# Fetching the first items' rows into buffers and later rows on top of positions in x, with reordered first steps

## The chip, the cores and the metric

One core of a Trainium2 chip runs the whole program. The time is what the device takes for one execution, in microseconds (us); of the kernel before three executions were timed, 1590.24, 1590.33 and 1594.37 us, median 1590.33.

## What is computed

A small language-model tower over 32 sequences of 256 tokens with 192 features. The part that matters here is the first one: the embedding with positions and four layers of a selective-scan block.

```python
x = embedding[tokens] + pos_enc[:S][None]
for l in range(L):          # L = 4
    h = _layernorm(x, g, bt)
    uv = h @ Wi.T + bi                    # u, v
    uc = _dwconv_causal(u, cw, cb)        # 4 taps
    delta = softplus(uc @ wd.T + bd_)
    Bm, Cm = uc @ wB.T + bB_, uc @ wC.T + bC_
    y = _selective_scan(uc, delta, Bm, Cm)   # h = h * exp(-delta) + uc * Bm;  y = sum(h * Cm)
    x = x + ((y * sigmoid(v)) @ wo.T + bo)
```

An attention block with a partial rotary embedding and an int8 feed-forward layer follow; the change does not touch them.

## The kernel before

x stays on the chip for the whole program, 64 tiles of 128 tokens by 192 features. An **item** is four tiles, two sequences, in one layer; a layer has 16 items and the four layers 64, numbered through. Each engine runs its own program, and the programs are written as a software pipeline: step m works on several items at once, `at(lag)` being item m - lag. The helper `steps` writes the first six steps of a layer out, loops over pairs of steps, and writes the last ones out. The engines meet only at semaphores, and each engine takes its own instructions strictly in the order written.

What an item goes through, with its lag and its line: DVE measures mean and variance one step ahead (`statistics` L1424, `variance` L1439, lag -1); POOL computes the inverse deviation in seven small instructions (`inverse_deviation`, L479 to L491, lag -1); at lag 0 ACT rounds the scaled rows (`round_rows`, L1176), DVE makes what the rounding left (`rest_of_rows`, L1448) and POOL adds the output bias to the rows for later (`bias_rows`, L503). At lag 1 PE transposes them (L758) and ACT saves them (`save_turned`, L1166). At lag 2 PE makes u and v (`uv`, L697), ACT saves u and makes the convolution's first tap (L1116 to L1137), DVE adds the other three (`other_taps`, L1465), ACT rounds the result (`round_uc`, L1186 and L1189), DVE makes the rest (`rest_of_uc`, L1479 and L1474), and ACT makes the gates sigmoid(v) (`gates`, sv_l L1199 and sv_h L1202). PE's `uv` of the next item waits for those gates. At lag 3 come the decay on ACT (`decay`, L1147) and PE's products from uc (L706, L717); at lag 4 the recurrence on DVE (scans hs_h L1500 and hs_l L1509), the output product (L787) and the residual sum (L1537).

The rows of layer 0 come from DRAM. The table of token numbers is made by DVE and PE in the first 5 us. `index` (L414) copies four columns of it, `gather` (L419) issues four indirect transfers of 128 rows each from POOL's queue into a buffer `emb` (items 0 to 3 have buffers of their own, later ones take turns), and `place` adds the positions and writes x: on DVE (L1404) for items 0 to 3, on POOL (L437) for the others. POOL issues the gathers of the first four items one after the other, and only then computes item 0's inverse deviation. In its step it places item m + 2, copies the indices of m + 4 and gathers m + 3, ahead of `inverse_deviation` and `bias_rows`. Before the first step DVE scales and centres layer 0's weights (`centre_weights`, L1360), ACT rounds them (`round_weights`, L1103), and DVE makes their rests (L1380, L1383). SP's queue brings weights: w_o and the biases bo_row after the first two items' rows, other weights after six items, later layers' weights when their buffers are free.

```python
            for n in range(FIRST):
                wait(pool, s_idx4, n + 1)
                gather(n, n, n % 2)
...
            inverse_deviation(item(0))
```

## Time and profile before

| what | value |
|---|---|
| time, median of three | 1590.33 us |
| time of the profiled execution | 1598.23 us |
| its span | 1596.3 us |
| PE busy | 1506.3 us, 94% |
| DVE busy | 1349.4 us, 85% |
| ACT busy | 1241.8 us, 78% |
| POOL busy | 836.2 us, 52% |
| gathers, adding of positions on POOL | 64 transfers issued; 12 instructions |

Engines are PE (matmul), DVE (vector), ACT (scalar), POOL (GpSimd) and SP (the queue of plain transfers). Busy time is from start to end of the instructions of an engine, without the issuing of waits and registers. The profiled execution is one of its own; its time is 7.90 us above the median of the others, and its span leaves out 1.9 us of its time. In the 40 slices of the profile PE is busy over 90% of each from the third to the last but two, all but one of them, so an average over the span says little about the first 80 us, where PE stands in two slices at 20 and 60%. The rows below are therefore taken from short stretches.

### The profile page before, as it was taken

The page shows a single profiled execution, that of the slowest core. Times are in us where ns is not written, and L with a number is a line of the kernel's source. Part 1 is how long each engine was busy: PE and PEld are TensorE (multiplying, and loading weights), DVE is VectorE, ACT ScalarE, POOL GpSimd, SP SyncE. Part 2 cuts the span into 40 slices and gives each one's busy share as a digit, 9 for nine tenths or more (in the row PEclk, how much of TensorE's full clock was granted, in tenths as well). Part 3 has the DMA queues.
Part 4 walks back from the last instruction along what each step waited for, and adds up shares of the span by engine and source line. Part 5 has one row for each costly group of instructions (what it writes and reads, how often), then busy time and mean ns, then how long its engine had stood idle before and what let it go on. Part 6 is the DMA issues. An engine that isn't in the chain of part 4 may idle for free.

```text
span 1596.3 us, 36428 instructions
## 1 busy us (share of the span) xinstructions
PE 1506.3 (94%) x11313; PEld 1232.6 (77%) x11313; DVE 1349.4 (85%) x3201; ACT 1241.8 (78%) x2686; POOL 836.2 (52%) x1428
## 2 busy tenths in 40 slices
PE   2699999999999999999999998999999999999986
PEld 1588878888888888888888886677777777777763
DVE  4699999999999999999999886678888878888763
ACT  2688878888888888888888963777787877877762
POOL 7777755443334453333333236566666666666642
PEclk9799999999999999999999997999999999999996
DMA  5311100000000000000000000000000000000000
GB/s 111 80 29 30 30 23 34 1 34 0 0 1 1 1 1 0 0 1 1 1 1 0 1 1 1 2 8 12 12 10 15 11 11 10 10 10 15 11 12 25
DMA packets 16571, 22.41 MB, mean 14 GB/s; under 512 B 2912, under 2 KB 13792, under 8 KB 16480
## 3 DMA queue, kind: packets, MB, share of 16 engines
q1 hardware_dynamic: 13408, 14.98, 2.8%
q0 software_dynamic: 3072, 6.30, 2.6%
q8 instruction: 48, 0.79, 0.2%
q14 instruction: 43, 0.35, 0.1%
HBM read 14.58 MB, written 6.29 MB: 13 GB/s over the span
## 4 chain that ended last, share of the span: by engine, by line
PE 60%; DVE 18%; ACT 9%; issue 9%; POOL 2%; DMA 1%; DVEq 1%; ACTq 0%; POOLq 0%
PE banks L706 9%; PE banks L921 7%; PE banks L697 7%; PE banks L889 6%; PE banks L846 5%; PE banks L873 5%; PE banks L860 4%; DVE hs_h L1500 3%; DVE x L1537 3%; DVE xs L1448 2%; PE banks L787 2%; PE banks L717 2%; PE banks L832 2%; PE banks L945 2%; PE banks L835 2%
## 5 line engine op out<-in xcount | busy, mean ns | idle before, releaser
L1593 DVE TENSOR_REDUCE mx<-banks 128x4 f32<-128x1024 f32 x192 | 234.2, 1220 | 45.6 <-PE banks L860 45.1
L1224 ACT ACTIVATE probs<-banks 128x1024 f32<-128x1024 f32 x192 | 195.7, 1019 | 84.5 <-PE banks L873 81.1
L503 POOL TENSOR_TENSOR x<-x,bo_row 128x768 f32<-128x768 f32 (+1 forms) x64 | 118.3, 1848 | 159.0 <-DVE ucr_r L1474 159.0
L697 PE MATMUL banks<-ht,w_uv 128*128 128x512 f32 x576 | 166.3, 398 | 14.3 <-ACT sv_l L1199 12.5
L479 POOL TENSOR_TENSOR lnt<-mv,const 128x4 f32<-128x4 f32 x64 | 20.4, 319 | 269.1 <-DVE mv L1439 268.8
L1465 DVE SCALAR_TENSOR_TENSOR uc_h<-u_h,vec,uc_h 128x512 f32<-128x512 f32 x192 | 146.9, 765 | 0.9 <-ACT uc_h L1137 0.9
L697 PEld LDWEIGHTS banks<-ht,w_uv 128*128 128x128 f32 x576 | 108.4, 191 | 42.0 <-issue 18.1
L1448 DVE SCALAR_TENSOR_TENSOR xs<-x,rstd,xs 128x192 fp32r<-128x192 f32 x256 | 89.9, 413 | 46.5 <-ACT xs L1176 46.5
L697 PE MATMUL banks<-ht,w_uv_rest 128*128 128x512 f32 x384 | 120.0, 394 | 0.0
L1116 ACT ACTIVATE u_l<-banks,vec 64x256 f32<-64x256 f32 x128 | 60.0, 469 | 73.5 <-PE banks L697 72.7
L873 PE MATMUL banks<-q_t,k_t 64*128 64x256 f32 x768 | 108.8, 334 | 7.7 <-ACT probs L1224 6.3
L706 PE MATMUL banks<-ucr_h,w_z 128*128 128x512 f32 x256 | 107.6, 420 | 4.5 <-issue 2.8
L846 PE MATMUL banks<-identr,parts 128*128 128x128 f32 x768 | 105.0, 261 | 4.2 <-issue 3.3
L1465 DVE SCALAR_TENSOR_TENSOR uc_l<-u_l,vec,uc_l 128x256 f32<-128x256 f32 x192 | 95.2, 496 | 12.1 <-POOL rstd L491 3.9
L1166 ACT ACTIVATE ht<-banks 128x512 fp32r<-128x512 f32 x192 | 100.8, 598 | 5.0 <-PE banks L758 3.5
L889 PE MATMUL banks<-probs,v_aug 128*32 128x256 f32 x1536 | 104.5, 390 | 0.0
L1133 ACT ACTIVATE uc_l<-banks,vec 64x256 f32<-64x256 f32 x128 | 71.7, 560 | 42.1 <-DVE inp_l L1494 41.0
L758 PEld LDWEIGHTS banks<-identr,xs 128*128 128x128 f32 x768 | 74.5, 142 | 38.0 <-DVE xs L1448 19.1
L1176 ACT ACTIVATE xs<-x,rstd 128x192 fp32r<-128x192 f32 (+1 forms) x256 | 95.6, 445 | 9.9 <-POOL rstd L491 8.3
L758 PE MATMUL banks<-identr,xs 128*128 128x128 f32 x768 | 77.6, 247 | 27.2 <-DVE xs L1448 19.0
L860 PE MATMUL banks<-k_t,q_t 64*128 64x256 f32 x768 | 94.7, 303 | 6.6 <-DVE mx L1593 2.6
L706 PE MATMUL banks<-ucr_l,w_z 128*128 128x512 f32 x256 | 101.0, 394 | 0.0
(191 smaller groups left out, 4662.8 us busy)
## 6 DMA issues: line engine op xcount, KB each, us to landing
out_dram<-y_out SPq DMA_DIRECT2D x32, 192.0 KB, 2.0
raw_z<-w_z_dram SPq DMA_DIRECT2D x4, 704.0 KB, 5.3
raw_uv<-w_uv_dram SPq DMA_DIRECT2D x4, 576.0 KB, 3.9
emb<-embedding_dram,idx POOLq DMA_INDIRECT x64
q_t<-mx_t SPq DMA_DIRECT2D x64, 6.0 KB
emb<-w_qkv_dram SPq DMA_DIRECT2D x1, 864.0 KB
w_o<-w_o_dram SPq DMA_DIRECT2D x1, 768.0 KB
bo_row<-bout_dram SPq DMA_DIRECT2D x4, 96.0 KB
```

What stands on the lines that cost most here:

```text
L503: nc.gpsimd.tensor_tensor(rows, rows, bo_row[:, l, :][:, None, :].broadcast_to([P, CT, D]), ALU.add).then_inc(x_biased, 1)
L697: last = nc.tensor.matmul(out[:], w, r[:], start=(k == 0), stop=(k == len(passes) - 1))
L706: last = nc.tensor.matmul(out[:], w, r[:, b, :], start=(k == 0), stop=(k == len(passes) - 1))
L758: last = nc.tensor.transpose(B_T[g][:, k * P:(k + 1) * P].bitcast(F32R), xs[:, k, g * P:(g + 1) * P], identr[:])
L846: last = nc.tensor.transpose(B_HEADS[g][:, (2 * o + t) * P:(2 * o + t + 1) * P].bitcast(F32R), parts[:, s, t, o, 2 * g:2 * g + 2, :].rearr ...
L860: last = nc.tensor.matmul(B_S[j][:, t * S:(t + 1) * S], q_t[q, s, g, t * P:(t + 1) * P], k_t[q, s, g, :], start=True, stop=True)
L873: last = nc.tensor.matmul(B_ST[j][:, t * S:(t + 1) * S], k_t[q, s, g, t * P:(t + 1) * P], q_t[q, s, g, :], start=True, stop=True)
L889: last = nc.tensor.matmul(bank[32 * h:32 * h + 32, c:c + S], v_aug[:, s, t, 4 * p + h, :], probs[:, (s + p) % 2, h // 2, (2 * (h % 2) + t) ...
L1224: act.activation(probs[:, (s + g // 2) % 2, g % 2, :].rearrange("p (j k) -> p j k", j=2), B_SST, ACT.Exp, scale=float(DH) ** -0.5).then_in ...
L1448: last = nc.vector.scalar_tensor_tensor(out=xs[:, k, D:2 * D], in0=x[:, tile_of(c, k)], scalar=rstd[:, s, k:k + 1], in1=xs[:, k, 0:D].bitc ...
L1465: nc.vector.scalar_tensor_tensor(out=uc, in0=uk, scalar=v(l, part, V_W0 + k), in1=uc, op0=ALU.mult, op1=ALU.add).then_inc(taps, 1)
L1593: nc.vector.tensor_reduce(mx[:, s].rearrange("p t (j h) -> p j t h", j=2)[:, :, :, g], B_SS.rearrange("p j (t k) -> p j t k", t=2), AX, AL ...
```

## The change

Four things. **Rows:** the index copies go; each gather reads its indices from the table itself. Items 0 to 3 are gathered into buffers as before, and DVE adds their positions. For items 4 to 15 SP first writes the positions into x, a transfer within the chip's memory, and POOL's gather then adds the embedding rows to what stands there; `place` on POOL is gone. POOL's part of layer 0 is written out in full. **POOL's opening:** the inverse deviation of item 0 comes after two items' gathers, and the other fetches are spread over the steps. **First steps:** in steps 0 to 4 of layer 0 DVE has an order of its own, with the measuring of later items behind the taps, and in steps 0 to 3 ACT computes the gates before it rounds uc. ACT rounds item 0 before the first step, and the wait for the weights' rests is split in two. **Table and bias:** an activation of one column loads the sigmoid's table at the start; the bias for layer 0 is one transfer, those of the other layers are sent later, last before the later weights; in the first four items POOL's bias waits for one item of uc more.

```diff
+        def items_of(t, n):
+
+            return t[:, n * CT * D:(n + 1) * CT * D].rearrange("p (b d) -> p b d", b=2)
+
+        positions = pos[:].rearrange("p h d -> p (h d)")[:, None, :].broadcast_to([P, 2, 2 * D])
...
-        def steps(eng, step):
+        def steps(eng, step, fetches=False):
 
 
             LEAD = 6
             for l in range(L):
-                for k in range(LEAD):
+
+                for k in range(NCH if fetches and l == 0 else LEAD):
                     m = l * NCH + k
                     step(lambda lag, m=m: item(m - lag), l, k)
+                if fetches and l == 0:
+                    continue
...
-            for n in range(2):
-                sp.wait_ge(s_emb[n], 16 * CT)
+
+            def base(n):
+
+                s = n % 2
+                wait(sp, xs_ready, n - 5)
+                wait(sp, s_base[s], 8 * (n - s - FIRST))
+                sp.dma_start(items_of(x, n), positions).then_inc(s_base[s], 16)
+
+
+
+            sp.wait_ge(s_pos, 16)
+            base(FIRST)
+            sp.wait_ge(s_first[1], 16 * CT)
+            sp.dma_start(bo_row[:, 0, :], bout[0:1, :].broadcast_to([P, D])).then_inc(s_bo[0], 16)
+            base(FIRST + 1)
+            sp.wait_ge(s_first[3], 16 * CT)
             sp.dma_start(w_o[:], w_o_d).then_inc(s_wo, 16)
-            for i in range(L):
-                sp.dma_start(bo_row[:, i, :], bout[i:i + 1, :].broadcast_to([P, D])).then_inc(s_wo, 16)
-
-            sp.wait_ge(x_loaded, 6)
+            for n in range(FIRST + 2, 10):
+                base(n)
+            for i in range(1, L):
+                sp.dma_start(bo_row[:, i, :], bout[i:i + 1, :].broadcast_to([P, D])).then_inc(s_bo[1], 16)
             for k, (lo, hi) in enumerate(((0, P), (P, D))):
                 sp.dma_start(w_out[0:hi - lo, k, :], w_out_d[lo:hi]).then_inc(s_w2, 16)
                 sp.dma_start(w_ffn_words[0:hi - lo, k, :], w_ffn_d[lo:hi]).then_inc(s_w2, 16)
@@ -370,11 +400,13 @@
             sp.dma_start(b_out[:], b_out_d.broadcast_to([P, D])).then_inc(s_w2, 16)
             sp.dma_start(b_ffn[:], b_ffn_d.broadcast_to([P, D])).then_inc(s_w2, 16)
             sp.dma_start(rope[:], rope_d).then_inc(s_w2, 16)
-            for l in range(1, L):
+            layer_loads(1)
+            for n in range(10, NCH):
+                base(n)
+            sp.wait_ge(x_placed, FIRST)
+            sp.dma_start(raw_qkv, w_qkv_d).then_inc(s_w2, 16)
...
-            def index(n, c, s):
-                e = n if isinstance(n, int) and n < FIRST else s
-                if not isinstance(n, int) or n >= FIRST:
-                    wait(pool, x_loaded, n - 1)
-                    wait(pool, s_idx4, n)
-                nc.gpsimd.tensor_copy(idx4[:, e, :], idx[:, bass.ds(c * CT, CT)]).then_inc(s_idx4, 1)
-
-            def gather(n, c, s):
-                e = n if isinstance(n, int) and n < FIRST else s
+            def fetch(n):
+                s = n % 2
+                if n >= FIRST:
+                    pool.wait_ge(s_base[s], 8 * (n - s - FIRST) + 16)
+
+                    wait(pool, s_rows[s], 8 * CT * (n - s - FIRST))
                 for k in range(CT):
-                    nc.gpsimd.indirect_dma_start(
-                        out=emb[:, e, k * D:(k + 1) * D], out_offset=None, in_=embedding,
-                        in_offset=bass.IndirectOffsetOnAxis(ap=idx4[:, e, k:k + 1], axis=0)).then_inc(s_emb[e], 16)
-
-            pool.wait_ge(s_idx, 2)
-            for n in range(FIRST):
-                index(n, n, n % 2)
-            for n in range(FIRST):
-                wait(pool, s_idx4, n + 1)
-                gather(n, n, n % 2)
-                if n == 1:
-                    for k, value in enumerate((EPS, -0.5, 1.5)):
-                        nc.gpsimd.memset(const[:, k, :], value).then_inc(s_zero, 1)
-                    pool.wait_ge(s_zero, 3)
-
-            def place(n, c, s):
-                wait(pool, x_loaded, n)
-                wait(pool, s_emb[s], 8 * CT * (n - s))
-                nc.gpsimd.tensor_tensor(
-                    x[:, bass.ds(c * CT * D, CT * D)].rearrange("p (b h d) -> p b (h d)", b=2, h=2),
-                    emb[:, s, :].rearrange("p (b h d) -> p b (h d)", b=2, h=2),
-                    pos[:].rearrange("p h d -> p (h d)")[:, None, :].broadcast_to([P, 2, 2 * D]),
-                    ALU.add).then_inc(x_loaded, 1)
+                    row = n * CT + k
+                    of_row = bass.IndirectOffsetOnAxis(ap=idx[:, row:row + 1], axis=0)
+                    if n < FIRST:
+                        nc.gpsimd.indirect_dma_start(out=emb[:, n, k * D:(k + 1) * D], out_offset=None, in_=embedding,
+                                                     in_offset=of_row).then_inc(s_first[n], 16)
+                    else:
+                        nc.gpsimd.indirect_dma_start(out=x[:, row * D:(row + 1) * D], out_offset=None, in_=embedding,
+                                                     in_offset=of_row, compute_op=ALU.add).then_inc(s_rows[s], 16)
...
+                if first_of_layer(it) and l < 2:
+                    pool.wait_ge(s_bo[l], 16 * (L - 1 if l else 1))
                 wait(pool, xs_ready, n + 1)
 
-                wait(pool, uc_ready, n - 1)
+                wait(pool, uc_ready, n if isinstance(n, int) and n < OPENING else n - 1)
...
+            pool.wait_ge(s_idx, 1)
+            fetch(0)
+            fetch(1)
+
+            pool.wait_ge(s_zero, 3)
             inverse_deviation(item(0))
+            fetch(2)
 
             def step(at, l, k):
-
-                def fetching(lag):
-                    it = at(lag)
-                    return it if it is not None and it[1] == 0 and (l > 0 or k is None or k - lag >= FIRST) else None
-
-                for lag, stage in ((-2, place), (-4, index), (-3, gather)):
-                    if (it := fetching(lag)) is not None:
-                        stage(it[0], it[2], it[3])
+                if l == 0 and k < OPENING:
+
+                    inverse_deviation(at(-1))
...
+            act.activation(table[:], ident[:, 0:1], ACT.Sigmoid)
...
+            round_rows(item(0))
...
+                if l == 0 and k is not None and k < OPENING:
+
+                    save_turned(at(1))
+                    decay(at(3))
+                    gates(at(2))
+                    round_uc(at(2))
+                    if k > 0:
+                        round_rows(at(0))
+                else:
+                    decay(at(3))
+                    save_turned(at(1))
+                    round_rows(at(0))
+                    round_uc(at(2))
+                    gates(at(2))
...
+                if l == 0 and isinstance(n, int) and n < FIRST:
+                    dve.wait_ge(x_placed, n + 1)
+                elif l == 0:
+                    wait(dve, s_rows[s], 8 * CT * (n - s - FIRST) + 16 * CT)
...
-            place(0)
-            rows_there(item(0))
-            statistics(item(0))
-            statistics_there(item(0))
-            variance(item(0))
-            place(1)
+            def place(n):
+                dve.wait_ge(s_first[n], 16 * CT)
+                nc.vector.tensor_tensor(items_of(x, n), emb[:, n, :].rearrange("p (b d) -> p b d", b=2), positions,
+                                        ALU.add).then_inc(x_placed, 1)
+
+            def measure(n):
+                if n < FIRST:
+                    place(n)
+                rows_there(item(n))
+                statistics(item(n))
+                statistics_there(item(n))
+                variance(item(n))
+
+            measure(0)
             centre_weights(0)
-            split_weights()
+            split_uv()
+            rest_of_rows(item(0))
+            measure(1)
+            split_z()
...
-                if l == 0 and k is not None and k + 2 < FIRST:
-                    place(k + 2)
+                if l == 0 and k is not None and k <= OPENING:
+
+                    if k == 0:
+                        nc.vector.memset(gain_rows[:], 1.0 / D).then_inc(mean_spread, 1)
+                        measure(2)
+                    other_taps(at(2), (0, 1, 2))
+                    rest_of_uc(at(2), 1)
+                    rest_of_uc(at(2), 0)
+                    if k == 1:
+                        rest_of_rows(at(0))
+                    elif k == 2:
+                        measure(3)
+                        rest_of_rows(at(0))
+                    elif k == 3:
+                        recurrence_products(item(0))
+                        rest_of_rows(at(0))
+                        recurrence_scan(item(0))
+                        recurrence_rest(item(0))
+                        measure(4)
+                    elif k == 4:
+                        save_y(at(4))
+                        residual(at(4))
+                        rest_of_rows(at(0))
+                        measure(5)
+                    return
```

ACT, from item 0's rows on. The names after the operation are output<-input: ht the transposed rows, ucr rounded uc, sv the gates. Before:

```order
L1166 ACTIVATE ht<-banks 128x512 x3
L1176 ACTIVATE xs<-x,rstd 128x192 x4
L1186 ACTIVATE ucr_l<-uc_l 64x256 x2
L1189 ACTIVATE ucr_h<-uc_h 128x512
L1199 ACT_TABLE_LOAD
L1199 ACTIVATE sv_l<-banks,vec 64x256 x2
L1202 ACTIVATE sv_h<-banks,vec 128x512
```

and in the change:

```order
L1195 ACTIVATE ht<-banks 128x512 x3
L1228 ACTIVATE sv_l<-banks,vec 64x256 x2
L1231 ACTIVATE sv_h<-banks,vec 128x512
L1215 ACTIVATE ucr_l<-uc_l 64x256 x2
L1218 ACTIVATE ucr_h<-uc_h 128x512
L1205 ACTIVATE xs<-x,rstd 128x192 x4
```

The gates moved from the end of the step to right behind the transposed rows, the rounding of the rows to the end, and the table load is no longer there.

POOL, its program behind the token table: idx are the indices, lnt and rstd the inverse deviation. Before:

```order
L414 COPY idx<-idx 128x4 x4
L419 DMA emb<-embedding_dram,idx 128x192 x8
L431 MEMSET const 128x4 x3
L419 DMA emb<-embedding_dram,idx 128x192 x8
L479 TENSOR_TENSOR lnt<-mv,const 128x4
```

and in the change:

```order
L458 MEMSET const 128x4 x3
L451 DMA emb<-embedding_dram,idx 128x192 x8
L496 TENSOR_TENSOR lnt<-mv,const 128x4
L498 TENSOR_TENSOR lnt<-lnt,const 128x4
L500 TENSOR_TENSOR lnt<-lnt 128x4
L502 TENSOR_TENSOR lnt<-lnt 128x4
L504 TENSOR_TENSOR lnt<-lnt,const 128x4
L506 TENSOR_TENSOR lnt<-lnt,const 128x4
L508 TENSOR_TENSOR rstd<-lnt 128x4
L451 DMA emb<-embedding_dram,idx 128x192 x4
```

Eight gathers and the copies no longer stand ahead of the inverse deviation.

DVE in step 3 of the change (inp, hs, hc belong to item 0's recurrence, xs to item 3's rows, stats and mv to item 4):

```order
L1528 SCALAR_TENSOR_TENSOR inp_h<-banks,vec,uc_h 128x512
L1531 SCALAR_TENSOR_TENSOR inp_l<-banks,vec,uc_l 128x256
L1481 SCALAR_TENSOR_TENSOR xs<-x,rstd,xs 128x192 x4
L1542 SCALAR_TENSOR_TENSOR hs_h<-dc_h,inp_h 128x256 x2
L1551 SCALAR_TENSOR_TENSOR hs_l<-dc_l,inp_l 128x256
L1556 SCALAR_TENSOR_TENSOR hc_h<-banks,vec,hs_h 128x512
L1560 TENSOR_TENSOR hc_l<-cb_l,hs_l 128x256
L1457 BN_STATS stats<-x 128x6 x4
L1472 BN_AGGR mv<-stats 128x2 x4
```

The rows of item 3 stand inside the recurrence of item 0, and the measuring of item 4 behind it; before, the measuring stood ahead of the taps, and the rows behind them.

## Rows read from the trace of the kernel before

**Rows 1.** Stretches: start:end us, length, then each engine's busy us, clock, DMA share, GB/s.
```profile
core 0 of [0], span 1596.3 us
...
0.00:34.15 34.15, 6.61 (x18) 4.17 (x18) 13.97 (x48) 5.90 (x11) 23.94 (x43) 1.00 0.62 128
34.15:98.25 64.10, 48.70 (x259) 41.77 (x260) 47.62 (x112) 46.78 (x95) 50.16 (x67) 0.87 0.28 62
98.25:198.25 100.00, 97.25 (x624) 85.84 (x623) 99.08 (x240) 83.37 (x169) 76.56 (x98) 1.00 0.17 29
198.25:273.34 75.09, 71.80 (x455) 62.09 (x454) 72.22 (x181) 61.32 (x125) 39.88 (x55) 1.00 0.09 30
286.90:360.30 73.40, 71.40 (x455) 62.13 (x454) 70.52 (x179) 61.68 (x127) 36.69 (x50) 1.00 0.05 19
428.87:442.45 13.58, 13.58 (x90) 12.09 (x90) 12.74 (x35) 11.68 (x25) 4.61 (x7) 1.00 0.00 0
```

**Rows 2.** Opening in time: start us, us, engine, line, out<-in, count [idle <-releaser].
```profile
4.89 0.64 POOL L414 COPY idx<-idx 128x4 int32<-128x4 int32 x4 [3.34 <-DVE idx L1341]
...
5.71 1.20 POOL L419 DMA_INDIRECT emb<-embedding_dram,idx  x1 [0.18 <-POOL idx L414]
...
13.40 0.96 DVE L1404 TENSOR_TENSOR x<-emb,pos 128x768 f32<-128x768 f32 x1 [8.15 <-DMA emb<-embedding_dram,idx]
...
15.49 0.95 POOL L419 DMA_INDIRECT emb<-embedding_dram,idx  x1 [0.31 <-issue]
15.57 0.38 DVE L1439 BATCH_NORM_AGGREGATE mv<-stats 128x2 f32<-128x6 f32 x4
...
18.93 0.96 DVE L1404 TENSOR_TENSOR x<-emb,pos 128x768 f32<-128x768 f32 x1 [2.98 <-DMA emb<-embedding_dram,idx]
...
19.81 1.66 DVE L1360 SCALAR_TENSOR_TENSOR raw_uv<-raw_uv,gain,banks 128x384 f32<-128x384 f32 x3
...
21.50 1.35 ACT L1103 ACTIVATE w_uv<-raw_uv 128x384 fp32r<-128x384 f32 x3 [11.32 <-DVE raw_uv L1360]
...
27.61 0.21 POOL L479 TENSOR_TENSOR lnt<-mv,const 128x4 f32<-128x4 f32 x1
...
30.93 0.20 POOL L491 TENSOR_TENSOR rstd<-lnt 128x4 f32<-128x4 f32 x1
...
32.69 1.40 DVE L1448 SCALAR_TENSOR_TENSOR xs<-x,rstd,xs 128x192 fp32r<-128x192 f32 x4 [0.98 <-ACT xs L1176]
...
34.15 1.76 PE L758 MATMUL banks<-identr,xs 128*128 128x128 f32 x12 [19.02 <-DVE xs L1448]
```

**Rows 3.** The same view, from PE's first products on.
```profile
37.67 1.62 PE L697 MATMUL banks<-ht,w_uv 128*128 128x512 f32 x3 [1.76 <-ACT ht L1166]
...
42.07 0.86 PE L697 MATMUL banks<-ht,w_uv 128*128 128x512 f32 x3
...
44.03 0.77 ACT L1137 ACTIVATE uc_h<-banks,vec 128x512 f32<-128x512 f32 x1
...
45.25 1.95 DVE L1465 SCALAR_TENSOR_TENSOR uc_l<-u_l,vec,uc_l 128x256 f32<-128x256 f32 x1 [3.85 <-POOL rstd L491]
...
52.68 1.28 ACT L1199 ACT_TABLE_LOAD   x1
...
55.08 1.62 PE L697 MATMUL banks<-ht,w_uv 128*128 128x512 f32 x3 [10.71 <-ACT sv_l L1199]
```

**Rows 4.** The same view: layer 0's step, then a scan in layer 1.
```profile
103.35 1.84 POOL L437 TENSOR_TENSOR x<-emb,pos 128x768 f32 x1
103.67 2.65 DVE L1500 TENSOR_TENSOR_SCAN hs_h<-dc_h,inp_h 128x256 f32<-128x256 f32 x2
...
106.14 1.04 POOL L419 DMA_INDIRECT emb<-embedding_dram,idx  x1 [0.43 <-issue]
...
106.24 0.66 DVE L1509 TENSOR_TENSOR_SCAN hs_l<-dc_l,inp_l 128x256 f32<-128x256 f32 x1
...
434.28 1.26 DVE L1500 TENSOR_TENSOR_SCAN hs_h<-dc_h,inp_h 128x256 f32<-128x256 f32 x2
```

63 lines of the change are left out of this document (31 added, 32 removed).

## The prediction

> **What bounds the kernel now.** I read the busy times by stretch first, since the change touches only the opening and layer 0. Between 428.87 and 442.45 us, one step deep in layer 1, PE is busy 13.58 of 13.58 us and DVE 12.74 [rows 1]: a steady step is PE's, about 13.7 us, and DVE has about 0.9 us to spare. In layer 0 from item 5 to item 12 (98.25 to 198.25 us) seven steps take 100.00 us, 14.29 each, with DVE busy 99.08 and PE 97.25 [rows 1]: there DVE sets the pace. In the first 34.15 us PE is busy 6.61 and DVE 13.97 us [rows 1]: nobody is the bound, a chain is. So the second view is the opening in order of time [rows 2]. Item 0's variances are ready at 15.95, yet POOL computes its inverse deviation only at 27.61, because the gathers of items 0 to 3 stand before it in POOL's program; ACT and DVE can round item 0 only then, and PE starts the first transposes at 34.15 after 19.02 us of idleness. The third view is the next stretch [rows 3]: PE stands 10.71 us before the second item's first product, which waits for ACT's gate sv_l; ACT computes the gates last in its step, behind a table load of 1.28 us and behind the rounding of uc. The fourth compares one DVE line in the two layers [rows 4].
>
> **The change, part by part.**
>
> *First item.* The four index copies and the wait around them go: the first gather starts at 4.9 in place of 5.71, so everything behind it is 0.8 us earlier; place starts at 12.6 in place of 13.40 and the variances, 2.55 us later as before, are there at 15.15 [rows 2]. The eight gathers of items 0 and 1 took from 5.71 to 16.44, 10.7 us [rows 2]; they now end at 15.6, and the inverse deviation of item 0 follows at once. It took 3.5 us (27.61 to 31.13) [rows 2], so rstd comes at 18.4 to 19.1; I take 18.4, because one of its links was slowed there by a DVE instruction. ACT is not late: DVE's centring begins when the variances are done, 15.15, and from its start (19.81) to the end of the rounding of w_uv (22.85) lie 3.0 us [rows 2], which gives 18.2. From rstd (31.13) to the transposes (34.15) there were 3.0 us, for the rounding of xs and its remainder [rows 2]: PE's first transposes start at 21.4, **12.7 us earlier**.
>
> *Steps 1 to 5.* Here the order of every engine is new, so I walked it through with the durations of the same lines. PE's transposes to the last first tap (uc_h, end 44.80) took 10.65 us [rows 2, 3], hence item 0's first taps are ready at 32.05. The marks are the starts of DVE's remainder of rows, the line at 32.69 before. Item 1: 28.4, released by the rows of item 2 (gathers issued 18.4 to 23.7, landed at 26.0, place and measure 2.5, overlapping a little). Item 2: 40.9, behind the taps of item 0, which POOL's bias holds up by about its own length (as the first tap took 1.95 us at 45.25 [rows 3]), their rounding, and the measuring of item 3. Item 3: 53, behind ACT's step, in which decay and gates now stand before the rounding of uc. Item 4: 68.5. Item 5: 84.5, against 98.25 [rows 1]. So **13.7 us** stand at item 5. The gates are early now: the second item's product starts near 34.3 in place of 55.08 [rows 3], 20 us ahead, but that lead is not kept, since DVE then waits for ACT's rounding of uc (about 3.7 us in step 3 and 2 in step 4) and carries the places and the two measures that step 3 holds. From the mark 45.25 (first tap) to 98.25 DVE needed 53.0 us; I give it 52.5. Bounds for this term: 12 us (the waits grow by 2) and 17 us (half of the waits vanish).
>
> *The table.* One activation with one column at the start brings the sigmoid table, and the load of 1.28 us at 52.68 goes. This is inside the marks above and adds nothing. From the load's start to the start of PE's product that waits for the gate behind it there are 2.40 us (52.68 to 55.08), the gate itself included [rows 3]. The Trainium skill (ScalarE: Activation LUTs, What ACT_TABLE_LOAD costs) adds a drain and puts each switch at about 2.66 us. By that page the removed load would give 1.4 us more than the row's; the row has no room for it, and the row decides.
>
> *Layer 0's steady steps.* POOL's place (1.84 us, L437) goes. In layer 0 the two scans of hs_h take 2.65 us where they take 1.26 in layer 1, and the scan starts 0.3 us after L437 does [rows 4]. Without place DVE needs 14.2 less 1.4, 12.8 us, and PE's 13.7 us are the bound again: 7 steps times 0.6 us is 4.1; the first of them still meets POOL's bias late, so **3.6 us**. Bounds 0 (another POOL instruction holds up the scan instead) and 4.1.
>
> *The step into layer 1.* Items 12 to 17 took 75.09 us; the same five steps of layer 1, without fetches, took 73.40 [rows 1]. The loads and splitting of weights stay, only two places and a few gathers go: **1.2 us**, bounds 0 and 1.7.
>
> *What comes in.* SP sends the positions into x, 12 transfers of 384 KB, each at least two steps before its rows; POOL's gathers then add. Nothing of before shows an adding gather. Its issue may cost as much as now (0.95 us and 0.30 between) or more; per step POOL has 5.3 us of gathers (eight in 10.7), 1.84 for bias, a tile of place's size, and 3.5 for the inverse deviation [rows 2, 4], 10.7 of 13.7, so 0.7 us more for each would still be hidden. Rows are asked for two steps after their issue, some 25 us; item 1's last gather was issued at 15.49 and its place began at 18.93 [rows 2], 3.4 us, and seven times that would still do. I take zero. The bias of item 0 waits only for one row of bo, sent when item 1's rows have landed (near 18.4), wanted at 32. w_o is sent near 34, wanted near 59. SP's queue has nobody else waiting.
>
> *Sum.* 13.7 + 3.6 + 1.2 = 18.5 us. The profiled execution had span 1596.3 and time 1598.2, 7.9 above the median of the runs; the edit should take the same from both. 1598.2 - 18.5 = 1579.7 for a profiled one, and **1590.3 - 18.5 = 1571.8** for the median. A difference under 0.3%, 4.8 us, is about what a measurement cannot tell from none.
>
> **Rivals.**
>
> 1. *The opening gains, layer 0's pace does not.* The gathers now begin right behind bias, under the scans. If they hold up two-input DVE instructions as place did, layer 0 keeps 14.29: gain 13.7, 1576.6 us. Against it: a gather runs at 106.14 under the scan hs_l, which takes its usual 0.66 us [rows 4]. The Trainium skill (SBUF — State Buffer, Who interferes with whom) says that a VectorE instruction with two SBUF inputs contends with a GpSimd instruction that reads SBUF; a gather reads its indices there, and by that rule this case would hold. Chance 0.17.
>
> 2. *PE is granted half its clock for longer.* At 37.67 three products take 1.62 us, at 42.07 they take 0.86 [rows 3]: PE was at the lower level, 1.2 GHz, when it first worked, and it fell again in this stretch (0.87 on average [rows 1]). If it stays low through steps 2 to 5, each step's 13.5 us of PE work at the upper level becomes longer than DVE's; the walk through gives item 5 at about 92 in place of 84.5: gain 11, 1579.3. Chance 0.10.
>
> 3. *The opening keeps more*: DVE's waits for ACT in steps 3 and 4 are shorter and the clock is at its upper level early: gain 22, 1568.3. Chance 0.12.
>
> 4. *Slower: the adding gathers make POOL the bound.* With d us from one gather to the next POOL's step is 4d + 5.3 us; it passes PE's 13.7 at d = 2.1, and over 12 items it eats all 18.5 us at d = 2.5. At d = 3 it costs 43 us and ends at 1571.8 + 43 = 1615. Only the transfer's kind speaks for it; today's d is 1.34 on average [rows 2]. Chance 0.04; another 0.03 for a d or a late landing that leaves no difference (1590).
>
> **How the numbers follow.** The forecast has 0.54, the rivals the rest. 0.54 + 0.17 + 0.10 + 0.12 is faster by over 4.8 us: 0.93; same 0.03; slower 0.04. The bounds of the terms are 12 and 22.8 us of gain, 1567.5 to 1578.3; rival 2 carries the upper end to 1581, rival 3 fits in. Range 1567 to 1581.
>
> **What would show it.** PE's first transposes at 21 to 22 us; no table load after the first; the second item's product near 34; DVE's remainder of item 5 near 84; hs_h pairs of 1.26 us in layer 0 and steps of 13.7; gathers 1.2 to 1.4 us apart on POOL with no DVE wait for them after item 3. I am wrong if DVE waits on rows in steps 3 to 15, if scans stay at 2.65, or if the lead at item 5 is under 12 us.

## The result and the profile after

The changed kernel takes 1586.84 us (median of 20 executions, 1583.19 to 1591.46). The kernel before, beside it on the same chip, took 1592.90 (20 executions). The ratio is 0.9965, 95% interval 0.9952 to 0.9977: faster by 6 us, a third of the forecast 18.5, and outside the range.

The two profiled executions also differ in the attention stage, which the change doesn't touch: behind item 63 the one before ran 679.9 us, the one after 677.2, and other kernels of this study 672 to 681. So I compare marks inside layers 0 and 1 and not spans. The same stretches of the kernel after, in the columns of [rows 1], cut at the starts of DVE's remainder of rows (line 1481) for items 5, 12 and 17:

```profile
0.00:22.45 22.45, 6.61 (x17) 4.17 (x17) 9.04 (x35) 5.98 (x12) 13.33 (x27) 1.00 0.66 147
22.45:93.64 71.19, 53.85 (x274) 44.62 (x274) 54.02 (x123) 45.17 (x94) 62.26 (x64) 0.90 0.48 105
93.64:192.83 99.19, 95.72 (x607) 84.60 (x608) 96.95 (x240) 82.88 (x168) 87.75 (x87) 0.98 0.32 59
192.83:267.50 74.67, 71.40 (x455) 62.15 (x454) 71.79 (x180) 61.65 (x126) 40.86 (x57) 1.00 0.07 21
```

PE starts 11.7 us earlier (22.45 against 34.15), near the forecast 12.7. Then the lead melts: from there to item 5 it needs 71.19 us where it took 64.10, items 5 to 12 take 99.19 instead of 100.00 (forecast 96.4), items 12 to 17 take 74.67 instead of 75.09 (forecast 73.9). The engine whose row changed is POOL: 87.75 busy of 99.19 us, where it had 76.56 of 100.00, although its placing is gone.

The marks of item n, from the traces, with three runs that are explained below (the forecast's for items 12 and 17 are the marks of before less 17.3 and 18.5 us, the sums of its terms so far):

```
item                         1      2      3      4      5     12     17
before                    38.9   51.7   68.2   84.0   98.2  198.2  273.3
forecast                  28.4   40.9   53.0   68.5   84.5  180.9  254.8
after                     30.9   43.0   56.1   73.8   93.6  192.8  267.5
plain gathers             31.7   43.9   55.5   72.5   87.5  183.8  257.3
DVE places                30.0   42.2   53.8   71.9   87.8  186.1  261.0
DVE bias, deviation first 31.3   42.4   54.6   70.2   84.8  186.0  271.3
```

The gathers of the two kinds in the kernel after (adding at line 454, plain at line 451), from the view of one line:

```profile
L454 POOL DMA_INDIRECT x<-embedding_dram,idx x48: 1536/1734/2737, 40.9 to 192.2; - x48
...
DMA to landing us min/median/max: 4.0/4.4/8.0
```
```profile
L451 POOL DMA_INDIRECT emb<-embedding_dram,idx x16: 942/954/1555, 4.9 to 33.4; - x16
...
DMA to landing us min/median/max: 3.4/4.4/5.5
```

An adding gather of 128 rows keeps POOL 1.54 to 2.74 us, 1.73 at the median, where a plain one keeps it 0.95. Inside an item the adding gathers start 2.05 us apart on average (1.83 to 2.49), where those of the kernel before start 1.34 apart. The software queue's rows of the two pages (packets, MB, share of the engines; after, then before) go with it:

```profile
q0 software_dynamic: 7680, 6.30, 3.2%
```
```profile
q0 software_dynamic: 3072, 6.30, 2.6%
```

The 64 plain gathers of before make 48 packets each; with the 16 that are still plain, 6912 packets are left for the 48 adding ones, 144 each, three times as many for the same bytes.

POOL from item 4's inverse deviation to item 5's, and DVE behind item 5's statistics (order of time; start us, us, engine, line, out<-in, count, [idle before <-releaser]):

```profile
68.15 0.20 POOL L508 TENSOR_TENSOR rstd<-lnt 128x4 f32<-128x4 f32 x1
68.85 1.62 POOL L454 DMA_INDIRECT x<-embedding_dram,idx  x1 [0.50 <-issue]
70.78 1.72 POOL L454 DMA_INDIRECT x<-embedding_dram,idx  x1 [0.31 <-issue]
...
75.68 2.42 POOL L520 TENSOR_TENSOR x<-x,bo_row 128x768 f32<-128x768 f32 x1
78.25 1.55 POOL L454 DMA_INDIRECT x<-embedding_dram,idx  x1 [0.16 <-issue]
...
85.28 0.80 POOL L496 TENSOR_TENSOR lnt<-mv,const 128x4 f32<-128x4 f32 x1
...
88.39 0.20 POOL L508 TENSOR_TENSOR rstd<-lnt 128x4 f32<-128x4 f32 x1
```
```profile
76.23 0.38 DVE L1472 BATCH_NORM_AGGREGATE mv<-stats 128x2 f32<-128x6 f32 x4
79.03 0.75 DVE L1528 SCALAR_TENSOR_TENSOR inp_h<-banks,vec,uc_h 128x512 f32<-128x512 f32 x1 [2.42 <-DMA x<-embedding_dram,idx]
...
82.82 1.14 DVE L1457 BATCH_NORM_STATS2 stats<-x 128x6 f32<-128x192 f32 x4
88.68 2.00 DVE L1498 SCALAR_TENSOR_TENSOR uc_l<-u_l,vec,uc_l 128x256 f32<-128x256 f32 x1 [4.72 <-issue]
```

Item 5's variances are ready at 76.6, and POOL turns to them at 85.28: the fetches of items 6 and 7 and a bias stand before them, back to back. DVE may overwrite the variances only when POOL has used them, and the wait for that stands ahead of its first tap. The view names no releaser for it, but the tap starts at 88.68, 0.1 us behind the end of POOL's last instruction: DVE stands 4.72 us. It waited 2.42 us for item 6's rows just before.

### The profile page after: what moved, and what is told of

Its sections match the earlier page's. It is cut to its first block, busy times and chain, and to the rows that moved or that the text cites. A ratio compares the mean times of both kernels' runs of the same rounds, so it can differ in the third digit from the quotient of the medians.

```text
span 1587.4 us, 36344 instructions
## 1 busy us (share of the span) xinstructions
PE 1507.7 (95%) x11313; PEld 1233.0 (78%) x11313; DVE 1347.7 (85%) x3200; ACT 1240.4 (78%) x2686; POOL 849.9 (54%) x1400
## 3 DMA queue, kind: packets, MB, share of 16 engines
q0 software_dynamic: 7680, 6.30, 3.2%
## 4 chain that ended last, share of the span: by engine, by line
PE 49%; DVE 20%; ACT 13%; issue 12%; POOL 4%; DVEq 1%; DMA 0%; ACTq 0%; POOLq 0%
PE banks L948 7%; PE banks L916 6%; PE banks L873 5%; PE banks L900 5%; PE banks L731 5%; DVE x L1579 4%; PE banks L887 4%; PE banks L722 4%; DVE xs L1481 3%; DVE hs_h L1542 3%; ACT xs L1205 3%; ACT ht L1195 2%; PE banks L859 2%; PE banks L972 2%; PE banks L862 2%
## 5 line engine op out<-in xcount | busy, mean ns | idle before, releaser
L722 PE MATMUL banks<-ht,w_uv 128*128 128x512 f32 x576 | 169.4, 403 | 16.5 <-ACT sv_l L1228 14.7
L496 POOL TENSOR_TENSOR lnt<-mv,const 128x4 f32<-128x4 f32 x64 | 28.2, 441 | 270.2 <-DVE mv L1472 270.2
L722 PEld LDWEIGHTS banks<-ht,w_uv 128*128 128x128 f32 x576 | 110.1, 194 | 45.3 <-issue 13.9
L1205 ACT ACTIVATE xs<-x,rstd 128x192 fp32r<-128x192 f32 (+1 forms) x256 | 95.7, 444 | 14.7 <-POOL rstd L508 13.2
L545 POOL TENSOR_TENSOR lnt<-mv,const 128x4 f32<-128x4 f32 x38 | 8.1, 213 | 174.1 <-DVE mv L1616 174.1
L731 PE MATMUL banks<-ucr_h,w_z_rest 128*128 128x512 f32 x256 | 100.5, 393 | 0.0
```

Source lines behind the costliest of these rows:

```text
L722: last = nc.tensor.matmul(out[:], w, r[:], start=(k == 0), stop=(k == len(passes) - 1))
L731: last = nc.tensor.matmul(out[:], w, r[:, b, :], start=(k == 0), stop=(k == len(passes) - 1))
L1205: last = act.activation(xs[:, k, 0:D], x[:, tile_of(c, k)], ACT.Identity, scale=rstd[:, s, k:k + 1])
```

## The experiments

Two theories at first. **A**: the adding gathers cost POOL issue time, and POOL's queue is the bound of the opening. **B**: they cost through late landing or through the DMA side. Each kernel was timed beside the kernel before, and ratios are to it; the kernels were timed in groups, so between two groups the ratios compare better than the times.

### Take the adding away

```diff
-  in_offset=of_row, compute_op=ALU.add).then_inc(s_rows[s], 16)
+  in_offset=of_row).then_inc(s_rows[s], 16)
```

> The changed kernel with the add taken out of the gathers of items 4 to 15: they overwrite x, so the positions of these items are left out of the result. All else is as in the change. Theory A (the adding gather is dear to issue: 1.93 us from one to the next on POOL against 1.25 for a plain one, and POOL sets the pace in steps 2 to 8): the gathers go back to 1.25 to 1.35, DVE's remainder of rows of item 5 starts near 84 in place of 93.6, items 6 to 9 come at 13.7 to 14.0 us instead of 14.3 to 14.8, item 16 near 244 in place of 253.9, and the time is 8 to 10 us below the change's, ratio to before about 0.990. Theory B (the new order of the first steps costs it, or landed rows are late; the issue price is hidden): item 5 stays at 91 to 94 and the time within 2 us of the change's, ratio 0.996. Theory C (PE's clock): item 5 stays and the granted clock in the first 100 us is as low as in the change.

1575.77 us, 0.9904 (0.9885 to 0.9924): 11 us less than the changed kernel, 10 by the ratios. The positions of items 4 to 15 are missing from its result, so it measures a price and is no kernel to use. The line's row in this kernel:

```profile
L454 POOL DMA_INDIRECT x<-embedding_dram,idx x48: 942/1024/1545, 41.7 to 179.7; - x48
...
DMA to landing us min/median/max: 3.4/3.7/5.5
```

Item 5 is rounded at 87.5, items 5 to 12 take 96.3 us (forecast 96.4) and items 12 to 17 take 73.5 (forecast 73.9). So the forecast's layer 0 exists as soon as the gathers cost what I had put. Both the issue and the landing (3.7 against 4.4 us) shrank, so A and B are not yet apart.

### Plain gathers, and POOL busy for the same time

Between plain gathers stand ten small POOL additions per item, into memory that nobody reads.

```diff
+  for j in range(2 + k % 2):
+      nc.gpsimd.tensor_tensor(spare[:, 10 * (n - FIRST) + 5 * k // 2 + j, :], const[:, 0, :], const[:, 1, :], ALU.add)
```

> The kernel of the run before with plain gathers in place of adding ones (items 4 to 15 are left without positions, 1575.8 us), with 10 small POOL additions of 128x4 per item put between those gathers, about 2.8 us per item, so that POOL's fetch of an item lasts as long as with adding gathers while the DMA side stays plain. Theory A (the issue time on POOL is what costs): 1585 to 1590 us, near the changed kernel's 1587, and items 4 and 5 begin as late as there. Theory B (the adding transfers land late or crowd the DMA engines, the issue time is only beside it): at most 3 us over the plain one, 1575 to 1579 us.

1583.41 us, 0.9940 (0.9923 to 0.9956): between the two, 7.6 of the 11.1 us. POOL's fetch of item 7 lasts from 76.64 to 83.7 us as it did from 78.25 to 85.3, and DVE again stands for item 5's deviation:

```profile
76.70 0.75 DVE L1531 SCALAR_TENSOR_TENSOR inp_h<-banks,vec,uc_h 128x512 f32<-128x512 f32 x1 [0.90 <-DMA x<-embedding_dram,idx]
...
86.48 1.99 DVE L1501 SCALAR_TENSOR_TENSOR uc_l<-u_l,vec,uc_l 128x256 f32<-128x256 f32 x1 [4.86 <-issue]
```

Issue time alone does about two thirds (by the marks of item 17, 257.3, 263.7 and 267.5, 6.4 of 10.2 us). Of the rest, 1.5 us is the wait for item 6's rows (2.42 us after, 0.90 here); it would be B's share.

### POOL's fetch behind the bias

`fetch(k + 3)` moved behind the inverse deviation and the bias, in every step.

> The changed kernel with each step's fetch moved behind the inverse deviation and the bias on POOL, so that no two fetches stand back to back between steps 3 and 4. Theory A says POOL's work per step is the same, only the doubled fetch ahead of item 5's inverse deviation goes: item 5 near 90 instead of 93.6, later steps as in the change, gain 1 to 3 us on the change. Theory B (order, not price) says that the 4.7 us which DVE waits at 83.9 for that inverse deviation go in full and stay gone: item 5 at 88 or 89 and the time 4 to 5 us below the change's.

1591.50 us, 0.9999 (0.9985 to 1.0012): neither theory's number. The order has a second side that I had not seen. Bias waits for DVE, and now the gathers wait with it:

```profile
72.36 1.83 POOL L520 TENSOR_TENSOR x<-x,bo_row 128x768 f32<-128x768 f32 x1 [3.99 <-DVE ucr_r L1507]
74.36 1.63 POOL L454 DMA_INDIRECT x<-embedding_dram,idx  x1 [0.16 <-issue]
```
```profile
84.16 0.75 DVE L1528 SCALAR_TENSOR_TENSOR inp_h<-banks,vec,uc_h 128x512 f32<-128x512 f32 x1 [7.28 <-DMA x<-embedding_dram,idx]
```

Item 6's rows are asked for 5.5 us later and DVE stands 7.28 us for them. The opening has no room there: in the changed kernel the first gather of item 6 is issued at 68.85, and DVE wants the rows at 76.6, 8 us later and not 25. Behind the opening this order does well: from item 6 to item 12 its steps are 13.7 us with adding gathers in place. POOL then waits 1.2 us for DVE before most biases, and every scan hs_l keeps its 0.66 us. So in a steady step the price of the adding gathers can be hidden, as the forecast had it; in the opening it isn't.

### Plain gathers with somebody placing

Complete kernels: plain gathers into four buffers for all items, no transfer of positions into x. DVE adds the positions (once per step, 0.95 us), or POOL does as before.

```diff
-  nc.gpsimd.indirect_dma_start(out=x[...], in_offset=of_row, compute_op=ALU.add)
+  nc.gpsimd.indirect_dma_start(out=emb[:, n % FIRST, ...], in_offset=of_row)
...
+  if l == 0 and k + 1 < NCH:
+      place(k + 1)
```

> All 16 items of layer 0 are gathered plainly into four buffers in turn, and DVE adds the positions (0.95 us each, behind the recurrence); no positions are sent by SP and nothing is added by a transfer. The result is complete. Theory A: POOL's gathers are cheap again and its place is gone, DVE's step is 12.8 + 0.9 = 13.7, equal to PE's: item 5 near 85, item 16 near 246, time 6 to 9 us below the change's, ratio to before 0.991. Theory B: item 5 at 91 or later, since the order of the first steps is the change's, and DVE's extra 0.9 us makes layer 0 slower: ratio 0.996 or above.

> The change's opening and orders, but items 4 to 15 gathered plainly into buffers and placed by POOL as before, ahead of the fetch in each step. POOL's step is then 1.84 for place and 5.2 for gathers against 7.7 for adding gathers: nearly the same load, with place under DVE's scans. Theory A: item 5 at 88 to 90, layer 0 at 14.2 to 14.3 us per step as before, item 16 near 253, ratio 0.996: no better than the change. Theory B (DMA landings of the adding gathers and of the positions are what is late): item 5 near 85 and item 16 near 248.

DVE placing: 1579.69 us, 0.9929 (0.9911 to 0.9947), faster than both kernels; steps of 14.0 us on average in items 5 to 12 and 13.8 from item 6 on. POOL placing: 1591.98, 0.9997 (0.9983 to 1.001), although the new order of the first steps is there in full. Item 5 is rounded at 92.2, the steps from item 7 to item 12 take 14.2 us, and the place falls on the scan again:

```profile
128.19 1.85 POOL L450 TENSOR_TENSOR x<-emb,pos 128x768 f32<-128x768 f32 x1
```
```profile
128.51 2.66 DVE L1537 TENSOR_TENSOR_SCAN hs_h<-dc_h,inp_h 128x256 f32<-128x256 f32 x2
```

### Single parts of the change

ACT's old order of the first steps in the changed kernel (gates last), the changed kernel without the early table load, and the kernel before with item 0's inverse deviation ahead of the fetches of items 2 and 3:

```diff
-  gates(at(2))
-  round_uc(at(2))
...
+  round_uc(at(2))
+  gates(at(2))
```
```diff
-  act.activation(table[:], ident[:, 0:1], ACT.Sigmoid)
```
```diff
+  first_deviation()
```

> The changed kernel with ACT's order of the first steps put back: decay, saved sums, rounding of rows, rounding of uc, gates last. Theory A (POOL is the bound of the opening, the gates' lead is lost again): the second item's product comes some 10 us later, and the whole run 1586 to 1591 us. Theory C (the early gates carry most of the gain that was measured): 1592 us or more, as the kernel before.

> The changed kernel without the one-column activation that brings the sigmoid table at the start. The load of 1.28 us then comes before the first gate. Own theory: it is off the path or costs its own length, 1586 to 1589 us. Rival: a switch costs more than its row (about 2.7 us and all of it on the path): 1589.5 us or more.

> The kernel before with one thing of the change: POOL computes item 0's inverse deviation behind the gathers of items 0 and 1 instead of behind those of items 0 to 3. Theory 1 (the first chain is what carries the opening): item 0's transposes start 8 to 12 us earlier and 6 or more of it is kept, 1583 to 1587 us. Theory 2 (the order of the next steps gives it back, gates last above all): under 3 us kept, 1589 to 1593 us.

Gates last (with decay ahead of the saved sums and the rounding of rows ahead of the gates): 1591.00 us, 0.9993 (0.9979 to 1.0006), about 4 us more than the changed kernel, so ACT's new order carries most of what was measured. The time stands at the upper end of what I had given to A (1586 to 1591), but it gives back most of the 6 us. The second item's product waits 10.50 us and starts at 44.97 instead of 36.82, and item 2 is rounded at 47.2 instead of 43.0. No table: 1585.91 us, 0.9955 (0.994 to 0.9969), no difference that can be told. The load stands at 36.30, before the first gate:

```profile
36.30 1.28 ACT L1227 ACT_TABLE_LOAD   x1
37.59 0.95 ACT L1227 ACTIVATE sv_l<-banks,vec 64x256 f32<-64x256 f32 x2
```

It is not absorbed at once: items 2 to 5 are rounded 0.8 to 1.3 us later than in the changed kernel, 0.4 of which stand at item 0 already. Behind item 5 shorter steps make that good; they come back below.

Early deviation alone: 1594.05 us, 1.0005 (0.9992 to 1.0017), and only 1.1 us of it reaches the transposes (33.04 against 34.15), because on DVE the measuring of a later item still stands before item 0's remainder:

```profile
29.27 0.96 DVE L1406 TENSOR_TENSOR x<-emb,pos 128x768 f32<-128x768 f32 x1 [3.83 <-DMA emb<-embedding_dram,idx]
...
31.61 1.38 DVE L1450 SCALAR_TENSOR_TENSOR xs<-x,rstd,xs 128x192 fp32r<-128x192 f32 x4
```

ACT had rounded item 0 from 22.69 on. The expectation of 8 to 12 us had not followed DVE's order. In the changed kernel, with both orders new, the transposes start at 22.45.

### POOL's order again, and the bias

Inverse deviation, fetch, bias in all of layer 0, in the changed kernel and in the kernel in which DVE places:

```diff
+  inverse_deviation(at(-1))
   if l == 0 and FIRST <= k + 3 < NCH:
       fetch(k + 3)
-  inverse_deviation(at(-1))
```

> The changed kernel, adding gathers kept, with POOL's order of the first four steps (inverse deviation, fetch, bias) kept through all of layer 0, so that item 5's inverse deviation doesn't stand behind eight adding gathers. Theory A (POOL's queue is late between 41 and 96 us, its order and load set when items 4 to 6 are rounded): item 5 is rounded 3 to 6 us earlier and 2 to 5 us of it is kept, 1582 to 1585 us. Theory D (POOL has too much work whatever its order, 13.1 us a step): the wait only moves to items 6 and 7 or to their rows, 1586 to 1590 us.

> The kernel with plain gathers into buffers and DVE placing each item (1579.7 us), with the same order on POOL through layer 0. Theory A: POOL has 10.4 us a step there, so its order costs little after item 6; 1576 to 1579 us. Theory D: no difference, 1579 to 1581 us; a loss if the rows of items 7 and later land late, 1582 us or more.

1594.91 us, 1.0016 (1.0003 to 1.0029), and 1601.57, 1.0057 (1.0043 to 1.0071). The first lies above both theories; the second only a loss by late rows could have covered, and rows aren't its cause. Item 5 comes at 89.7 instead of 93.6 as A said, and then from item 6 on every step is 15.0 us long (15.8 in the second). The reason stands in four rows of the first:

```profile
132.61 2.39 POOL L520 TENSOR_TENSOR x<-x,bo_row 128x768 f32<-128x768 f32 x1
136.33 0.35 POOL L496 TENSOR_TENSOR lnt<-mv,const 128x4 f32<-128x4 f32 x1 [1.33 <-DVE mv L1472]
```
```profile
132.69 2.61 DVE L1498 SCALAR_TENSOR_TENSOR uc_l<-u_l,vec,uc_l 128x256 f32<-128x256 f32 x1
135.88 0.37 DVE L1472 BATCH_NORM_AGGREGATE mv<-stats 128x2 f32<-128x6 f32 x4
```

The bias now lies under DVE's first tap, which takes 2.61 us instead of 0.48; the variances come behind the tap, POOL waits for them, and so its next bias is late by the same. In the second kernel it is the scan hs_l, 2.70 instead of 0.67. With the deviation first POOL starts each step behind DVE's variances, and the collision repeats in each of the six steps from item 6 to item 12.

That made me read where bias lies in the changed kernel, and in the one with plain gathers:

```profile
114.40 2.27 POOL L520 TENSOR_TENSOR x<-x,bo_row 128x768 f32<-128x768 f32 x1
```
```profile
114.95 2.27 DVE L1551 TENSOR_TENSOR_SCAN hs_l<-dc_l,inp_l 128x256 f32<-128x256 f32 x1
```
```profile
118.79 1.85 POOL L520 TENSOR_TENSOR x<-x,bo_row 128x768 f32<-128x768 f32 x1 [2.78 <-DVE ucr_r L1507]
```
```profile
122.10 0.67 DVE L1551 TENSOR_TENSOR_SCAN hs_l<-dc_l,inp_l 128x256 f32<-128x256 f32 x1
```

With adding gathers POOL comes 3 us late to its bias, and it lies under the scan hs_l in three steps of 14.4 us (items 6 to 9). From item 9 on it lies under hs_h instead, 2.24 us where it was 1.26, and the steps are 13.7 to 13.8. With plain ones POOL waits for DVE's ucr_r, the bias lies under instructions that read one operand from PSUM, and steps are 13.6. POOL's waits between 110 and 190 us (us in total, times, longest), in the changed kernel and with plain gathers:

```profile
POOL x L454 <- issue: 6.0, 22, 0.3
POOL x L454 <- DMA x<-pos: 0.2, 1, 0.2
```
```profile
POOL x L520 <- DVE ucr_r L1507: 16.8, 6, 2.8
POOL x L454 <- issue: 6.0, 22, 0.3
POOL lnt L496 <- DVE mv L1472: 1.3, 6, 0.2
```

So in the changed kernel POOL waits for no engine in these steps, where it has 18 us of waits with plain gathers: it isn't hidden there, it is level with PE. Where its bias falls hangs on shifts of a microsecond. In the kernel without the table, and in the one with a later transfer of positions (below), the adding gathers are in place, yet every hs_l keeps 0.67 us, since the bias starts just behind it, and items 5 to 12 take 97.3 us instead of 99.2.

### Bias off POOL

DVE adds the bias of layer 0 at the end of its step, adding gathers kept; then the same with the deviation first; and, for size, the changed kernel with item 5's deviation alone moved before its fetch.

```diff
+  if l == 0:
+      own_bias(at(0))        # adds bo_row by nc.vector
```

> The changed kernel, adding gathers kept, with the bias of layer 0 added by DVE at the end of its step (128x768, about 0.95 us) instead of by POOL (1.85 to 2.4 us). POOL then has about 11.3 us a step instead of 13.1, and no large POOL instruction is left to fall under a scan. Theory A (POOL's load in the opening, and its late bias over DVE's scans in items 5 to 9, are what the adding gathers cost): steps of 13.7 to 13.9 us from item 6 on and 1577 to 1582 us. Theory B (the late landing of adding gathers costs by itself): 1584 us or more.

> As the kernel in which DVE adds the bias of layer 0, and in addition POOL computes the inverse deviation before the fetch in every step. With POOL's bias alone this order made a loop of 15.0 us a step, in which bias lay under DVE's first tap. Theory A': without bias on POOL that loop can't form; item 5 is rounded at 88 to 90 us instead of 93.6 and steps are 13.7: 1574 to 1579 us. Rival: the loop is made by the gathers themselves (steps of 14.5 us or more, 1588 us or more).

> The changed kernel with one thing moved: in step 4 POOL computes item 5's inverse deviation before the fetch of item 7 instead of behind it. Theory A: item 5 is rounded 4 us earlier (89 to 90 us), later steps are as in the changed kernel; part of it is lost again at item 6, whose deviation now stands behind the fetches of items 7 and 8: 1583 to 1587 us. Rival (POOL's total load alone counts, the order nothing): 1587 us and more.

1592.03 us, 0.9999 (0.9987 to 1.0011); 1590.97, 0.9992 (0.9981 to 1.0004); 1584.64, 0.9960 (0.9948 to 0.9973). The first two times missed and lie where I had put the rivals, but the opening of the second speaks against B. With all gathers from item 4 on adding, its item 5 is rounded at 84.8 us, where the forecast had 84.5, since POOL gets to its deviation in time:

```profile
73.16 0.81 POOL L496 TENSOR_TENSOR lnt<-mv,const 128x4 f32<-128x4 f32 x1 [0.47 <-DVE mv L1472]
...
76.97 1.77 POOL L454 DMA_INDIRECT x<-embedding_dram,idx  x1 [0.50 <-issue]
```
```profile
84.85 1.41 DVE L1481 SCALAR_TENSOR_TENSOR xs<-x,rstd,xs 128x192 fp32r<-128x192 f32 x4 [0.78 <-ACT xs L1205]
...
89.21 0.95 DVE L1491 TENSOR_TENSOR x<-x,bo_row 128x768 f32<-128x768 f32 x1
```

What eats it are steps of 14.45 us, and items 12 to 17, in which DVE also prepares weights, take 85.3 us against 74.7. The 0.95 us on DVE alone don't explain the steps: from item 6 to item 12 DVE is busy 81.79 of 86.75 us here, and 81.77 of 82.53 us in the kernel in which it places, whose steps are 13.8. The bias stands at the end of DVE's step, and DVE waits 3.6 us for ACT's rounded rows in these six steps; which chain makes 14.45 I have not separated. The third: item 5's mark comes 5.2 us earlier, at 88.4, and item 6's only 1.8 us, 106.6 against 108.4, because its deviation now stands behind two fetches. Its time is 2.2 us lower, but the intervals of the two kernels overlap nearly in full, so only the marks show the gain.

### The opening relieved alone

DVE adds the bias of the first five (or six) items and POOL takes the deviation first there; everything later is as in the changed kernel. In a third kernel, also SP's first transfer of positions is sent behind item 1's rows; that was tried alone too.

```diff
+  EARLY_BIAS = 5             # 6 in the second
...
+  first = l == 0 and k < EARLY_BIAS
+  if first:
+      inverse_deviation(at(-1))
```

> The changed kernel, adding gathers kept, with POOL relieved in the first five steps only: DVE adds the bias of items 0 to 4, and POOL computes the inverse deviation before the fetch there; from step 5 on everything is as in the changed kernel. Theory A (the opening of the forecast is there as soon as POOL keeps up; later bias belongs to POOL, since on DVE it lengthens each step to 14.45 us): item 5 rounded at 85 us, steps of 13.7 to 14.1 from item 6, 1575 to 1580 us. Theory D (after the opening POOL falls behind again and its bias lies under the scans, 14.4 us a step): 1581 to 1585 us.

> The same with six steps instead of five, so that item 6's deviation too stands before its fetch. If the wait moves to item 6 in the five-step kernel, 1 to 3 us faster than that one; if not, 0 to 1 us slower for one more bias on DVE.

> The five-step kernel with SP's first transfer of positions sent behind item 1's rows. Item 0 is placed at 12.7 us instead of 14.0; 0.5 to 1.5 us faster than the five-step kernel if that lead is kept, the same if it is lost in the waits of items 1 to 4.

> The changed kernel with SP's first transfer of positions into x sent only when item 1's rows have landed. Theory: that transfer of 384 KB is what made item 0's rows come 1.4 us later than forecast; place of item 0 at 12.6 to 13.0 in place of 14.0 us and 0 to 1 us of the time, 1586 to 1587 us. Rival: other transfers delay them (weights, the index), place stays at 14.0 and the time at 1587 us.

Five steps 1584.63 us, 0.9943 (0.9922 to 0.9965); six steps 1580.03, 0.9915 (0.9898 to 0.9933); five steps with the later transfer 1587.72, 0.9960 (0.9945 to 0.9976); the later transfer alone 1584.03, 0.9957 (0.9942 to 0.9971). The five steps have the opening that A promised (item 5 at 84.3) and D's time. The six-step kernel, in the columns of the first fence, up to the marks of items 5, 12 and 17:

```profile
0.00:86.47 86.47, 56.47 (x272) 45.97 (x273) 58.64 (x163) 50.42 (x105) 63.30 (x84) 0.92 0.57 123
86.47:185.00 98.53, 98.52 (x630) 85.71 (x630) 96.69 (x240) 83.18 (x169) 86.45 (x87) 1.00 0.34 60
185.00:260.20 75.20, 71.35 (x453) 61.56 (x453) 72.29 (x181) 61.55 (x126) 43.49 (x58) 1.00 0.08 22
```

The whole kernel, adding gathers in place, runs 7 us below the changed one (8 by the ratios, and the intervals are apart): the lead of 11.8 us at item 5 is 13.2 at item 12. The five-step kernel needs 16.4 us from item 5 to item 6 where this one needs 14.4, so the wait had moved to item 6; between these two the intervals overlap, and the marks of item 17 stand 2.8 us apart. The transfer of 384 KB did delay item 0's rows (its place at 12.7 with the later transfer, 14.00 after, 13.40 before [rows 2]), but the 1.3 us are gone at item 1 (31.6 against 30.9), and they are no measurable time; the kernel with both does no better than without.

## Why the prediction was wrong

**First item.** Right within 1.1 us: transposes at 22.45, forecast 21.4. The difference comes from item 0's rows, placed at 14.00 where I had 12.6: the first transfer of positions runs at the same time. Sent later, it lets them be placed at 12.73, and the transposes start at 21.55. The prediction had costed that transfer at nothing.

**What comes in: "I take zero."** This is the step that failed. The working had the right formula, 4d + 5.3 us for POOL's step, and took d as it was, 1.34. It is 2.05 on average, so POOL's step is 13.5 by that formula, just under PE's 13.7: by my bound still hidden. The bound was the second half of the mistake. It compared POOL's load with a *steady* step, and it was asked of an opening in which POOL does each thing just when it is wanted and runs behind. There each gather's price is paid: the eight gathers between the deviations of items 4 and 5 keep POOL 13.9 us from its next work in the changed kernel and 9.9 with plain gathers, the eight before them 14.7 and 10.7, and the mark of item 5 moved by 6.2 us between the two kernels. In the prediction's own words, that 0.7 us more for each "would still be hidden" is what failed. The 25 us between issue and use were wrong for the same reason: POOL is so late there that 8 are left.

**Steps 1 to 5.** With plain gathers item 5 is at 87.5, 3 us behind my walk, all of it already there at item 1 (31.7 against 28.4); from item 1 to item 5 they need 55.8 us, forecast 56.1. With POOL relieved it is 84.8. The 2.5 us at item 1 of the changed kernel are POOL's as well, in two ways that end together. Item 2's rows, whose gathers ran from 19.59 to 25.3 us (18.4 to 23.7 in the walk), were placed by DVE at 28.01 (26.0) and measured at 30.6. Last, by 0.3 us, came ACT's rounding of item 1, which had waited until 29.3 for item 1's inverse deviation, and that stands behind the same gathers; the walk had named the rows alone. 1.2 us of it are the later start, which item 0 handed on. So in sum the walk over DVE, ACT and PE held, and POOL was the engine on which it was too short. That the relieved kernel comes within 0.3 us of the forecast is in part luck: its item 1 is 2.9 us late as well, and items 1 to 5 take 53.5 us instead of 56.1. In sum the opening gained 4.6 instead of 13.7. With plain gathers the whole kernel is 16.5 us below the one before, where the forecast had 18.5, so this one term carries most of the miss.

**Layer 0's steps.** With plain gathers the scans hs_h take 1.26 us, as forecast, and the seven steps 96.3 us. The change got 99.2. In three of its steps POOL's late bias lies under the other scan, which makes 2.3 of the 2.9 us; in the last three it lies under hs_h, which takes 2.24 us, but these steps are only 0.1 us longer than with plain gathers. That is rival 1 in its effect but not in its cause: it blamed gathers. A gather that lies beside DVE's taps, which read two operands from SBUF, did not lengthen them: at 118.95 POOL issues one and at 119.68 DVE's uc_h tap takes its usual 0.75 us. The Trainium skill (SBUF — State Buffer, Who interferes with whom) describes the contention between a two-input VectorE instruction and GpSimd's reads of SBUF; the rows agree for additions over 128x768 (beside a bias 0.67 becomes 2.27 to 2.70 us, beside a place a pair of scans of 1.26 becomes 2.66), and not for this gather, which reads its indices.

**The step into layer 1.** Plain gathers 73.5 us (forecast 73.9), after 74.7. The padded kernel, with POOL as busy, took 73.5 too, so it isn't POOL's load alone; the 1.2 us lie between items 12 and 13, where a scan and a tap are longer in the changed kernel (2.83 and 1.49 us for 2.23 and 0.74), and why stays open.

**The table.** Nothing in the time, as forecast; the run without it can't be told apart.

**Rivals.** The mechanism of rival 4 was the right one, at a price just below its threshold: it was to begin at 2.1 us between gathers, the condition of a steady step, and at 2.05 the adding had already taken 11 of the 18.5 us. I gave 0.07 to everything in which the adding costs POOL something, and that number had no row behind it, only the absence of one. Two of my own signs of being wrong came: the lead at item 5 under 12 us, and DVE's wait for item 6's rows. Rival 2: the granted clock was 0.90 in the opening against 0.87 [rows 1]. Behind item 5 it is 0.98 where it was 1.00, from a stretch at 0.66 between 95 and 100 us; there DVE is busy 4.94 of 5.00 us and sets the pace, so I see no part of the loss in it.

Open stays how the last 3.4 us between the padded kernel and the changed one divide: 1.5 us is the wait for item 6's rows, the rest may lie in the longer bias or in gathers of up to 2.74 us. By the marks 2.2 us are there at item 5, 2.6 at item 12 and 3.8 at item 17. That late landing costs the opening nothing once POOL keeps up is shown by item 5 at 84.8.

## What to carry to other kernels

An operation that no trace shows deserves a term with a range, not zero; an accumulating gather saves an addition, but on the engine that issues it the price here was some 0.7 us each. For the four of an item POOL needed 7.5 us on average until its next instruction instead of 5.4 with plain ones, 2.1 us more, to save a placing of 1.85 us. Before calling an engine hidden because its load is below the step, look at the stretch in which the order of its queue decides: an engine that is nearly as full as the step has no place where a late start is caught up. And where a shared engine's large instruction lies relative to the others' is part of the schedule; a bias that came 3 us late here cost 0.7 us in each of three steps.

## What the runs showed that I had not expected

- A software-queue gather that adds takes 1.54 to 2.74 us of POOL where the plain one takes 0.95 us, and 144 packets where that takes 48: 7680 against 3072 in the whole kernel, for the same 6.30 MB.
- A POOL addition over 128x768 beside a DVE instruction with two operands in SBUF lengthens that one: the tap from 0.48 to 2.6 us, the scan from 0.67 to 2.7. The addition is mostly longer too, 2.3 to 2.4 us for 1.85, though not always (1.84 at 156.19, beside hs_h). If the late one feeds the other, the collision can repeat in every step: 15.0 and 15.8 us for 13.7.
- The best complete kernels tried are plain gathers with DVE placing, 1579.69 us, and the relieved opening of six steps with adding gathers, 1580.03; neither can be told from the other, and both beat the changed kernel, by 7 us in the times and by 6 and 8 in the ratios.
